# One change to a four-layer attention kernel: its hand-made order is laid out with other costs and constraints, and the rows of maxima travel in two transfers instead of four

## The chip, the cores and the metric

The kernel runs on one core of one Trainium2 chip. The time is the device time of one execution in microseconds, and the number to predict is the median over several executions of the changed kernel. The engines are TensorE (PE in the profile, its weight loads PEld), VectorE (DVE), ScalarE (ACT), GpSimd (POOL) and SyncE (SP), which here only issues transfers.

## The reference

The input x is [4, 2048, 256] in fp32. Four layers follow, each with a residual and a layer norm without parameters:

```
x = x + attn0(norm(x))      # one head, key and value width 64, causal, T = 2048, biases
x = x + ffn0(norm(x))       # fp8-quantised input and weight, 256 -> 256, plus bias
x = x + attn1(norm(x))      # 16 heads of width 16, rotary embedding, causal
x = x + ffn1(norm(x))       # sigmoid(xr Wr) * (relu(xk Wk)^2 Wv), xr and xk mix x with the row before
```

Causal softmax takes scores minus the row's maximum. The 16-head attention over 4 x 2048 positions is most of the work.

## The kernel before, in words

The sequence is cut into 16 chunks of 512 positions (4 batches x 4). Each chunk has a first stage (layer norms 0, 1 and 2, the single-head attention, the fp8 layer, the projections Q, K and V of the 16-head attention, rotary embedding, and the writing of Q, K and V to DRAM), and a last stage (output projection, layer norm 3, the last layer). Between them lie 64 blocks (batch, group of 4 heads, chunk of queries) of the 16-head attention. A block first makes the scores with queries on the partitions, only to find each row's maximum: TensorE writes them into PSUM (job `max`, L1905 and L1912) and VectorE reduces them (`max d`, L1639 and L1643). The maxima are joined and split in two fp16 parts (`nmax`, L1652, L1655, L1656), turned by TensorE (`turnmax`, L1922), copied to SBUF (`turnmax d`, L1668) and sent by SyncE into two extra contraction rows of the query tile `qst` (`rows`, L1096). Then TensorE makes the scores with keys on the partitions, the maximum already subtracted by those extra rows (`scores`, L1937 and L1944), ScalarE takes the exponential (`exp`, L1402), and TensorE multiplies by the values (`values`, L1959).

A layer norm is three jobs: `stats` on VectorE (L1501, L1504), `root` on GpSimd (L1186, L1188), `norm` on VectorE: four tensor_scalar instructions of 128x256 from SBUF to SBUF (L1523). `mix` (L1694) is two instructions with two SBUF operands. GpSimd adds biases (L1200 `bias0`, L1230 `bias`), sums probabilities (`sum0`, L1216 to L1224), finishes the rotary embedding (`roped`, L1242), squares (L1270) and adds residuals (L1237, L1275). After four of the first `root` jobs GpSimd also fills the key tiles (`pool.memset(kst...)`, L1193, eight instructions); these belong to no job.

Order. When the program is built, `schedule()` lays out some 10,000 jobs by a greedy simulation: `Order.run` calls `go` for each stretch of 3 us, with a random set of weights on the kinds of job drawn from the next number of the list `SEEDS`. In `go` each engine takes, of the jobs that are possible now, the one of lowest key plus weight. A job has an engine, a key, a time for which it holds its engine, a latency `lat` until its successors see it, the jobs it comes after, and what PSUM banks it takes or frees. The result is one fixed list of jobs for each engine, and the program emits instructions in exactly that order, with semaphore waits only for data and buffers. So an engine never passes over a job that isn't ready. The planned times themselves appear nowhere in the program, save in `repeats()`, which puts filler matmuls (L1727) where TensorE is planned to be idle for long.

SyncE issues all transfers of the main part from one queue in its own planned order. `put` (L1054, three transfers) and `put v` (L1060, four) write Q, K and V to DRAM, `load k`, `load q` (L1080, two each) and `load v` (L1088, one) read them back, `load x` (L1003) brings the next chunk.

Of the kernel before, what the change touches and what calls it, by code (L numbers as in the profile page):

```python
# [241 lines left out]
def max_pieces(i, c, g):  # L242
# [3 lines left out]
    if c == i // TPC and i % TPC == 1:  # L246
# [25 lines left out]
SEEDS = (405, 334, 333, 23, 291, 224, 511, 412, 119, 511, 511, 412, 255, 426, 355, 304, 119, 477, 180, 347, 49,  # L272
# [40 lines left out]
FAR_M, FAR_S = 2, 2  # L313
scored, paired = [], []


class State:


    def __init__(self, left, listed, jobs):  # L320
        self.left = left
        self.ready = {e: [] for e in ("PE", "DVE", "ACT", "POOL", "SP")}
        for name in listed:
            if not left[name]:
                self.ready[jobs[name][0]].append(name)
        self.ready_at = dict.fromkeys(listed, 0.0)
        self.free_at = dict.fromkeys(self.ready, 0.0)
        self.order = {e: [] for e in self.ready}
        self.vacant = [0.0] * 8
        self.home, self.tenants, self.start = {}, {}, {}  # L330
        self.now, self.mode, self.todo = 0.0, None, len(listed)


class Order:
# [47 lines left out]
    def go(self, state, then, number, until, weights, stick, patience):  # L382
# [4 lines left out]
        now, mode, todo = state.now, state.mode, state.todo  # L387

        def possible(name):

            at, claim = ready_at[name], jobs[name][5]
            if claim == "D":
                return max(at, min(max(vacant[n], vacant[n + 1]) for n in HOMES[claim]))
            return max(at, sorted(vacant[n] for n in HOMES[claim])[claim == "E"]) if claim else at

        while todo and now < until:
            nxt = 1e18
            moved = False
            for e in ready:
# [45 lines left out]
                free_at[e] = end  # L445
                if free:
# [14 lines left out]
        state.now, state.mode, state.todo = now, mode, todo  # L461


def chunk_jobs(o, b, q):
# [25 lines left out]
    add("SP", "load x", c, key() - (60.0 if b else 1e4), 0.1, ("store x2", p2), ("norm", p2 and (2, *p2)), lat=9.0 if c == (0, 1) else 4.0)  # L490
# [28 lines left out]
    add("SP", "rows0", c, key(), 0.2, ("turnmax0 d", c), ("rows0", p), last, lat=2.9)  # L519
# [34 lines left out]
    add("SP", "store x2", c, key(), 0.1, ("addf", (*c, 0)), ("addf", (*c, 1)), lat=3.0)  # L554
# [8 lines left out]
    for bl in range(4):  # L563
# [5 lines left out]
        add("SP", "put", (*c, bl), key(0.9), 0.5, ("res", (*c, bl)), lat=4.0)  # L569
# [3 lines left out]
    add("SP", "put v", c, key(), 0.4, ("v1", (*c, 0)), ("v1", (*c, 1)), lat=4.0)  # L573
# [8 lines left out]
def head_jobs(o, b, hg, q):  # L582
# [4 lines left out]
    for load in KEYS.loads(*me):  # L587
        old = KEYS.old[load]
        add("SP", "load k", load, pos - LEAD - 25, 0.15, ("put", (b, load[3], 2 * (hg // 2) + 1)),
            *[job for reader in (KEYS.readers(old) if old else []) for job in scored_with(*reader)], lat=4.5)  # L590
    slot = block_before(b, hg, q, QRING)
    add("SP", "load q", me, pos - LEAD - 25, 0.15, ("put", (b, q, 2 * (hg // 2))),
        *(scored_for(*slot) if slot else []), lat=4.5)
    for load in VALUES.loads(*me):
        old = VALUES.old[load]
        add("SP", "load v", load, pos - 25, 0.1, ("put v", (b, load[3])),
# [21 lines left out]
    add("SP", "rows", me, end - 20, 0.3, ("turnmax d", me), lat=2.6)  # L618
# [27 lines left out]
    add("SP", "put att", me, end + 2, 0.1, ("out", me), lat=3.0)  # L646


def tail_jobs(o, b, q):
# [12 lines left out]
    add("SP", "load x2", c, key(), 0.1, ("store x2", c), ("store y", p2),  # L662
        *[("put", (0, NQ - 1, bl)) for bl in (2, 3) if c in ((0, 0), (0, 1))], lat=4.0)
    add("SP", "load att", c, key(), 0.1, *[("put att", (b, hg, q)) for hg in range(NHG)],
# [38 lines left out]
    add("SP", "store y", c, key(), 0.1, ("addv", (*c, 0)), ("addv", (*c, 1)), lat=3.0)  # L703
# [107 lines left out]
def build(nc, x_in, y_out, w):  # L811
    ctx = ExitStack()
    with ctx:
# [81 lines left out]
        nmaxb = sb("nmaxb", [P, MAXROWS, 2, HG // 2, TPC], F16)  # L895
# [72 lines left out]
        def rows_written(wt, b, hg, q):  # L968
            n = block_no(b, hg, q)
            wt.wait_ge(f"rows {n % QRING}", 64 * (n // QRING + 1))  # L970
# [23 lines left out]
        def _(sp):  # L994
# [24 lines left out]
            for kind, item in ORDER["SP"]:  # L1019
# [70 lines left out]
                elif kind == "rows":  # L1090
                    n = block_no(*item)
                    wt.job("turnmax d", item)
                    for odd in range(2):
                        for row in range(MAXROWS):
                            at = 8 * (2 * row + odd)
                            sp.dma_start(qst[HALF * odd + PROWS + row:HALF * odd + PROWS + row + 1, n % QRING, :, :],  # L1096
                                         nmaxT1[at:at + 8, n % 2, :]).then_inc(S[f"rows {n % QRING}"], 16)
# [347 lines left out]
        def _(dve):  # L1445
# [36 lines left out]
            for kind, item in ORDER["DVE"]:  # L1482
# [163 lines left out]
                elif kind == "nmax":  # L1646
# [4 lines left out]
                    for odd in range(2):  # L1651
# [3 lines left out]
                    link(dve.tensor_scalar(nmaxb[:, 0, :, :, :], nmax1[:, :, :, :], 1.0 / UNIT1, None, ALU.mult))  # L1655
                    ins = dve.scalar_tensor_tensor(out=nmaxb[:, 1, :, :, :].rearrange("p o g t -> p (o g t)"),  # L1656
                                                   in0=nmax1[:, :, :, :].rearrange("p o g t -> p (o g t)"), scalar=1.0 / UNIT1,
# [396 lines left out]
```

## Time and profile before

| | |
|---|---|
| median of 3 runs | 2310.23 us (2308.37 to 2310.39) |
| the profiled execution's own time | 2312.3 us |
| its span, first to last instruction | 2310.4 us |
| granted TensorE clock, mean | 0.993 |
| SyncE transfers of the rows of maxima (L1096) | 256, of 2 KB each |

The span is 1.9 us less than the profiled execution's own time, and that time is 2.1 us over the median. Engine busy shares are averages over the whole span. A matmul's end is modelled by the profiler, so a busy TensorE isn't TensorE at its peak. In the rows below an instruction group of the timeline is merged: "1.38 ... x4" is 1.38 us from the first start to the last end of four instructions. A bracket at the end is the idle time of that engine before the group and what ended it.

### The profile page before, as it was taken

The page shows a single profiled execution, that of the slowest core. Times are in us where ns is not written, and L with a number is a line of the kernel's source. Part 1 is how long each engine was busy: PE and PEld are TensorE (multiplying, and loading weights), DVE is VectorE, ACT ScalarE, POOL GpSimd, SP SyncE. Part 2 cuts the span into 40 slices and gives each one's busy share as a digit, 9 for nine tenths or more (in the row PEclk, how much of TensorE's full clock was granted, in tenths as well). Part 3 has the DMA queues.
Part 4 walks back from the last instruction along what each step waited for, and adds up shares of the span by engine and source line. Part 5 has one row for each costly group of instructions (what it writes and reads, how often), then busy time and mean ns, then how long its engine had stood idle before and what let it go on. Part 6 is the DMA issues. An engine that isn't in the chain of part 4 may idle for free. (4 is left out here: it accounts for less than half of the span.)

```text
span 2310.4 us, 50495 instructions
## 1 busy us (share of the span) xinstructions
PE 2207.4 (96%) x19196; PEld 1022.9 (44%) x19196; DVE 2005.4 (87%) x4326; ACT 1506.5 (65%) x2753; POOL 529.9 (23%) x528
## 2 busy tenths in 40 slices
PE   7799999999999999999999999999999999999998
PEld 4455543343444444443354545444354444342444
DVE  6678999998988998898998989899988899999942
ACT  2234567767756777766846677667675677778764
POOL 6454220212223020312124112230222300000012
PEclk9999999999999999999999999999999999999999
DMA  2412312120211221120121212122021131010110
GB/s 52 120 59 72 109 37 77 34 65 15 60 45 47 75 73 50 54 71 15 51 68 47 76 50 80 33 59 58 20 68 55 32 90 53 21 43 25 30 49 30
DMA packets 185883, 125.29 MB, mean 54 GB/s; under 512 B 84912, under 2 KB 185392, under 8 KB 185648
## 3 DMA queue, kind: packets, MB, share of 16 engines
q1 hardware_dynamic: 184880, 121.16, 18.9%
q8 instruction: 157, 2.57, 0.5%
q10 hardware_dynamic: 768, 0.92, 0.1%
q14 instruction: 78, 0.64, 0.1%
HBM read 62.20 MB, written 59.24 MB: 53 GB/s over the span
## 5 line engine op out<-in xcount | busy, mean ns | idle before, releaser
L1639 DVE TENSOR_REDUCE mx<-psum 128x1 f32<-128x512 f32 (+2 forms) x2304 | 1291.3, 621 | 87.0 <-PE psum L1905 55.2
L1402 ACT ACTIVATE probs<-psum 128x512 f32<-128x512 f32 x2176 | 1136.1, 609 | 316.2 <-PE psum L1937 185.4
L1959 PE MATMUL psum<-probs,vs 128*17 128x512 f32 (+3 forms) x5120 | 573.7, 535 | 1.2 <-ACT probs L1402 1.0
L1905 PE MATMUL psum<-kst,qst 48*128 48x512 f16 (+3 forms) x2560 | 428.1, 350 | 26.8 <-DVE mx L1639 12.8
L1937 PE MATMUL psum<-qst,kst 50*128 50x512 f16 (+3 forms) x2560 | 419.7, 350 | 27.9 <-DVE mx L1639 7.7
L1905 PEld LDWEIGHTS psum<-kst,qst 48*128 48x128 f16 x2560 | 127.3, 93 | 346.8 <-ACT probs L1402 131.3
L1937 PEld LDWEIGHTS psum<-qst,kst 50*128 50x128 f16 x2560 | 125.0, 93 | 306.2 <-ACT probs L1402 115.4
L1959 PEld LDWEIGHTS psum<-probs,vs 128*17 128x17 f32 x5120 | 96.6, 96 | 165.9 <-issue 139.7
L1912 PE MATMUL psum<-maskq,identh 64*128 64x128 bf16 (+1 forms) x2048 | 125.2, 202 | 0.0
L1186 POOL TENSOR_SCALAR vare<-mv 128x4 f32<-128x4 f32 x64 | 14.6, 229 | 471.7 <-DVE mv L1504 471.7
L1944 PE MATMUL psum<-maskk,identh 64*128 64x64 bf16 (+1 forms) x2048 | 113.0, 202 | 0.0
L1944 PEld LDWEIGHTS psum<-maskk,identh 64*128 64x128 bf16 x2048 | 95.3, 95 | 33.3 <-issue 0.7
L1912 PEld LDWEIGHTS psum<-maskq,identh 64*128 64x128 bf16 x2048 | 95.6, 95 | 31.4 <-issue 0.6
L1872 PE MATMUL psum<-wqk,xnT 128*128 128x512 f32 x224 | 104.5, 604 | 1.3 <-DVE roped L1622 0.9
L1275 POOL TENSOR_TENSOR xp<-xp,gate 128x512 f32<-128x512 f32 x32 | 40.7, 1275 | 228.9 <-DVE gate L1702 228.9
L1242 POOL TENSOR_TENSOR roped<-rcos,roped 128x512 f32<-128x512 f32 x56 | 72.8, 1307 | 87.9 <-DVE roped L1622 87.9
L1356 ACT ACTIVATE probs<-psum 128x1024 f32<-128x1024 f32 x48 | 49.1, 1023 | 66.8 <-PE psum L1813 66.4
L1523 DVE TENSOR_SCALAR xn<-xs,mv,rstd 128x256 f32<-128x256 f32 x192 | 85.4, 506 | 6.4 <-POOL rstd L1188 6.0
L1643 DVE TENSOR_REDUCE mx<-psum 128x2 f32<-128x512 f32 x128 | 82.7, 681 | 8.3 <-PE psum L1912 8.1
L1501 DVE BATCH_NORM_STATS2 stats<-xs 128x6 f32<-128x256 f32 x192 | 67.0, 410 | 24.1 <-DMA xs<-x_in 13.6
L1222 POOL TENSOR_TENSOR sums<-sums,probs 128x512 f32<-128x512 f32 (+1 forms) x64 | 72.4, 1131 | 64.8 <-ACT probs L1356 42.9
L1745 PE MATMUL psum<-ident,xn 128*128 128x128 f32 x512 | 69.1, 281 | 14.3 <-DVE xn L1523 13.9
(173 smaller groups left out, 2757.4 us busy)
## 6 DMA issues: line engine op xcount, KB each, us to landing
qk_dram<-parts SPq DMA_DIRECT2D x168, 128.0 KB
qst<-qk_dram SPq DMA_DIRECT2D x128, 96.0 KB, 2.3
kst<-qk_dram SPq DMA_DIRECT2D x128, 96.0 KB, 2.3
v_dram<-vst SPq DMA_DIRECT2D x64, 136.0 KB, 4.0
vs<-v_dram SPq DMA_DIRECT2D x64, 136.0 KB, 2.1
xs<-x_in SPq DMA_DIRECT2D x16, 512.0 KB, 3.9
x_dram<-xs SPq DMA_DIRECT2D x16, 512.0 KB, 3.2
att_dram<-ast SPq DMA_DIRECT2D x64, 128.0 KB, 2.0
```

The source lines that it names most:

```text
L1222: pool.tensor_tensor(sums0[:, off:CH], sums0[:, off:CH], even, ALU.add).then_inc(S["chain s"], 1)
L1242: pool.tensor_tensor(into[:, t, :], rcos[:, t % 2, :], into[:, t, :], ALU.add).then_inc(S["roped"], 1)
L1402: act.activation(dst, src, ACT.Exp, scale=DK1 ** -0.5 / LIFT ** 2).then_inc(S["exp"], 1)
L1523: ins = dve.tensor_scalar(dst[:, t, :], src[:, t, :], mv[:, at, t, 0:1], rstd[:, at, t:t + 1], ALU.subtract, ALU.mult)
L1639: ins = dve.tensor_reduce(mx1[:, n % 2, 2 * g + odd, tile % TPC, c:c + 1], bank(src, at, at + cols), AX.X, ALU.max)
L1643: ins = dve.tensor_reduce(mx1[:, n % 2, odd:HG:2, i % TPC, c], tiles(bank(src, 0, cols * len(pieces)), cols), AX.X, ALU.max)
L1872: ins = pe.matmul(home(kind, item), xnTs[lane(b, q)][:, c, P * t:P * (t + 1)], wqk1[:, c, :], start=(c == 0), stop=(c == DC - 1))
L1905: ins = pe.matmul(two[odd][:, at:at + cols], qst[rows, qslot, pair, P * (tile % TPC):P * (tile % TPC + 1)], kst[rows, kslot, pair, 0:cols] ...
L1912: ins = pe.matmul(two[odd][:, at + cols - P + HALF * part:at + cols], identh[rows, part, :], maskq[rows, part, HALF * part:P], start=False ...
L1937: ins = pe.matmul(two[odd][:, at:at + cols], kst[rows, kslot, pair, keys], qst[rows, qslot, pair, CH - cols:CH], start=True, stop=not diag ...
L1944: ins = pe.matmul(two[odd][:, at:at + upto], identh[rows, part, :], maskk[rows, part, 0:upto], start=False, stop=(part == 1))
L1959: ins = pe.matmul(bank(7, off, CH, rows=VW, row=32 * h), vtile[:, h, :], probs[:, HG * (step_no(b, hg, k) % PSTEPS) + h, at:at + CH - off] ...
```

## The change

Three things are changed. First, the order's constraints: VectorE jobs of the kinds in `SHARED` (`norm`, `mix`, `nmax`) are possible only when GpSimd is free in the plan, and GpSimd jobs are possible only after the last of those has ended (`port`). Nothing of this is a wait in the program; it only moves jobs in the lists. Second, the time for which a transfer job holds SyncE in the plan. Third, the rows of maxima: the fp16 parts are laid out as (odd, part, head pair x tile), so that one transfer of 16 source rows writes both extra rows of a half of `qst`. `SEEDS` is another list (753 numbers for 752), so the order of all jobs on all engines is another one.

```diff
+SHARED = ("norm", "mix", "nmax")
...
         def possible(name):
 
             at, claim = ready_at[name], jobs[name][5]
+            if name[0] in SHARED and jobs[name][0] == "DVE":
+                at = max(at, free_at["POOL"])
+            if jobs[name][0] == "POOL":
+                at = max(at, port)
...
                 end = start + time
                 free_at[e] = end
+                if e == "DVE" and name[0] in SHARED:
+                    port = end
...
-    add("SP", "load x", c, key() - (60.0 if b else 1e4), 0.1, ...
+    add("SP", "load x", c, key() - (60.0 if b else 1e4), 0.45, ...
-    add("SP", "rows0", c, key(), 0.2, ..., lat=2.9)
+    add("SP", "rows0", c, key(), 1.35, ..., lat=2.9)
-        add("SP", "put", (*c, bl), key(0.9), 0.5, ("res", (*c, bl)), lat=4.0)
+        add("SP", "put", (*c, bl), key(0.9), 1.87, ("res", (*c, bl)), lat=3.0)
-    add("SP", "put v", c, key(), 0.4, ..., lat=4.0)
+    add("SP", "put v", c, key(), 2.1, ..., lat=4.0)
-        add("SP", "load k", load, pos - LEAD - 25, 0.15, ...   # load q alike
+        add("SP", "load k", load, pos - LEAD - 25, 0.85, ...
-        add("SP", "load v", load, pos - 25, 0.1, ...           # store x2, put att, load x2, load att, store y alike
+        add("SP", "load v", load, pos - 25, 0.45, ...
-    add("SP", "rows", me, end - 20, 0.3, ("turnmax d", me), lat=2.6)
+    add("SP", "rows", me, end - 20, 1.35, ("turnmax d", me), lat=2.1)
...
-        nmaxb = sb("nmaxb", [P, MAXROWS, 2, HG // 2, TPC], F16)
+        nmaxb = sb("nmaxb", [P, 2, MAXROWS, HG // 2 * TPC], F16)
...
                     for odd in range(2):
-                        for row in range(MAXROWS):
-                            at = 8 * (2 * row + odd)
-                            sp.dma_start(qst[HALF * odd + PROWS + row:HALF * odd + PROWS + row + 1, n % QRING, :, :],
-                                         nmaxT1[at:at + 8, n % 2, :]).then_inc(S[f"rows {n % QRING}"], 16)
+                        first = HALF * odd + PROWS
+                        sp.dma_start(qst[first:first + MAXROWS, n % QRING, :, :],
+                                     nmaxT1[16 * odd:16 * (odd + 1), n % 2, :]).then_inc(S[f"rows {n % QRING}"], 16)
...
-                    link(dve.tensor_scalar(nmaxb[:, 0, :, :, :], nmax1[:, :, :, :], 1.0 / UNIT1, None, ALU.mult))
-                    ins = dve.scalar_tensor_tensor(out=nmaxb[:, 1, :, :, :]..., in0=nmax1..., in1=nmaxb[:, 0, :, :, :]...,
+                    of = nmax1[:, :, :, :].rearrange("p o g t -> p o (g t)")
+                    link(dve.tensor_scalar(nmaxb[:, :, 0, :], of, 1.0 / UNIT1, None, ALU.mult))
+                    ins = dve.scalar_tensor_tensor(out=nmaxb[:, :, 1, :], in0=of, scalar=1.0 / UNIT1, in1=nmaxb[:, :, 0, :],
                                                    op0=ALU.mult, op1=ALU.subtract)
```

The semaphore of a block's rows now counts to 32 instead of 64, and the transpose of `nmaxb` reads the new layout.

## Rows read from the trace of the kernel before

**Rows 1.** The page, part 1: busy us, share of the span, instructions.
```profile
PE 2207.4 (96%) x19196; PEld 1022.9 (44%) x19196; DVE 2005.4 (87%) x4326; ACT 1506.5 (65%) x2753; POOL 529.9 (23%) x528
```
**Rows 2.** Stretches: us, busy PE, PEld, DVE, ACT, POOL, PEclk, DMA share, GB/s.
```profile
0.00:200.00 200.00, 166.74 (x1043) 93.96 (x1043) 138.77 (x327) 59.51 (x86) 105.65 (x124) 0.94 0.28 75
200.00:2200.00 2000.00, 1942.33 (x17515) 877.08 (x17515) 1829.52 (x3916) 1386.87 (x2559) 403.74 (x384) 1.00 0.19 53
```
**Rows 3.** Stretches, line L1523 (norm) alone: us, busy DVE, PEclk, DMA share, GB/s.
```profile
0.00:200.00 200.00, 32.87 (x44) 0.94 0.28 75
200.00:2310.00 2110.00, 84.76 (x212) 1.00 0.19 52
```
**Rows 4.** Timeline, VectorE: a norm with nothing beside it, one with company.
```profile
95.82 1.38 DVE L1523 TENSOR_SCALAR xn<-xs,mv,rstd 128x256 f32<-128x256 f32 x4
46.79 5.91 DVE L1523 TENSOR_SCALAR xn<-xs,mv,rstd 128x256 f32<-128x256 f32 x4 [1.48 <-POOL rstd L1188]
```
**Rows 5.** Timeline, GpSimd, beside that second norm.
```profile
46.71 1.84 POOL L1193 MEMSET kst<- 128x1024 f16 x2
48.51 1.30 POOL L1216 TENSOR_TENSOR sums<-probs 128x512 f32<-128x512 f32 x1
...
51.30 1.26 POOL L1224 TENSOR_TENSOR sums<-sums,probs 128x512 f32<-128x512 f32 x1
```
**Rows 6.** Groups by line: mix and the fp16 part of the maxima.
```profile
L1694 DVE SCALAR_TENSOR_TENSOR xrk<-x3T,mu,xrk 128x512 f32<-128x512 f32 x64 | 47.8, 790 | 13.2 <-ACT xrk L1423 13.2
L1655 DVE TENSOR_SCALAR nmaxb<-nmax 128x16 f16<-128x16 f32 x64 | 17.6, 275 | 2.2
```
**Rows 7.** The same lines: ns minimum/median/maximum of one instruction.
```profile
L1694 DVE SCALAR_TENSOR_TENSOR xrk<-x3T,mu,xrk x64: 729/742/1749, 327.2 to 2294.2; 128x512 f32<-128x512 f32 x64
L1655 DVE TENSOR_SCALAR nmaxb<-nmax x64: 174/175/2257, 134.3 to 2215.7; 128x16 f16<-128x16 f32 x64
```
**Rows 8.** Line L1193, the key tiles' filling.
```profile
L1193 POOL MEMSET kst<- x8: 951/951/952, 22.4 to 74.2; 128x1024 f16 x8
```
**Rows 9.** Timeline, VectorE and GpSimd: GpSimd starts inside VectorE's job.
```profile
977.09 3.43 DVE L1523 TENSOR_SCALAR xn<-xp,mv,rstd 128x256 f32<-128x256 f32 x4
977.25 2.46 POOL L1200 TENSOR_TENSOR xs<-xs,boc 128x1024 f32<-128x1024 f32 x1 [1.01 <-DVE xn L1523]
```
**Rows 10.** Timeline, SyncE, 92 to 112 us.
```profile
95.57 3.97 SPq L1054 DMA_DIRECT2D qk_dram<-xp  x6
99.64 2.09 SPq L1080 DMA_DIRECT2D qst<-qk_dram  x4
...
105.57 1.85 SPq L1080 DMA_DIRECT2D kst<-qk_dram  x4
107.51 0.40 SPq L1003 DMA_DIRECT2D xs<-x_in  x1
```
**Rows 11.** Timeline, VectorE and TensorE, what waits for that load.
```profile
101.73 1.15 DVE L1561 TENSOR_REDUCE mx<-psum 128x1 f32<-128x384 f32 x2
112.75 1.40 DVE L1501 BATCH_NORM_STATS2 stats<-xs 128x6 f32<-128x256 f32 x4 [9.88 <-DMA xs<-x_in]
115.86 1.22 PE L1872 MATMUL psum<-wqk,attT 128*128 128x512 f32 x1 [9.01 <-DVE xrk L1622]
```
**Rows 12.** Timeline, SyncE: one block's rows (L1096), one chunk's (L1039).
```profile
1032.93 2.72 SPq L1096 DMA_DIRECT2D qst<-nmaxT  x4
249.50 1.35 SPq L1039 DMA_DIRECT2D nm<-nmaxT  x2
```
**Rows 13.** Waits of TensorE: total us, times, longest.
```profile
PE psum L1745 <- DVE xn L1523: 13.9, 6, 4.0
PE psum L1905 <- DVE mx L1639: 12.8, 37, 2.0
PE psum L1937 <- DMA qst<-nmaxT: 4.5, 6, 1.2
```

More of the change, by code:

```diff
@@ L269 @@
 STRETCH, AMPLITUDE = 3.0, 60.0
-SEEDS = (405, 334, 333, 23, 291, 224, 511, 412, 119, 511, 511, 412, 255, 426, 355, 304, 119, 477, 180, 347, 49,
[35 rows of a table removed]
+SEEDS = (158, 23, 200, 40, 361, 477, 216, 312, 314, 23, 426, 121, 412, 283, 327, 412, 412, 427, 157, 41, 180,
[35 rows of a table added]
 HOMES = {"D": (0, 2, 4), "E": (0, 1, 2, 3, 4, 5, 6), "P": (6, 5, 4, 3, 2, 1, 0), "O": (6,), "V": (7,)}
 FAR_M, FAR_S = 2, 2
+SHARED = ("norm", "mix", "nmax")
 scored, paired = [], []
@@ L330, in __init__ @@
         self.home, self.tenants, self.start = {}, {}, {}
-        self.now, self.mode, self.todo = 0.0, None, len(listed)
+        self.now, self.mode, self.todo, self.port = 0.0, None, len(listed), 0.0
 class Order:
@@ L386, in go @@
         vacant, home, tenants, order = state.vacant, state.home, state.tenants, state.order
-        now, mode, todo = state.now, state.mode, state.todo
+        now, mode, todo, port = state.now, state.mode, state.todo, state.port
         def possible(name):
             at, claim = ready_at[name], jobs[name][5]
+            if name[0] in SHARED and jobs[name][0] == "DVE":
+                at = max(at, free_at["POOL"])
+            if jobs[name][0] == "POOL":
+                at = max(at, port)
             if claim == "D":
@@ L460, in go @@
                 now = max(now, nxt)
-        state.now, state.mode, state.todo = now, mode, todo
+        state.now, state.mode, state.todo, state.port = now, mode, todo, port
 def chunk_jobs(o, b, q):
@@ L488, in both @@
         return (("turned", (ln, *c)),)
-    add("SP", "load x", c, key() - (60.0 if b else 1e4), 0.1, ("store x2", p2), ("norm", p2 and (2, *p2)), lat=9.0 if c == (0, 1) else 4.0)
+    add("SP", "load x", c, key() - (60.0 if b else 1e4), 0.45, ("store x2", p2), ("norm", p2 and (2, *p2)), lat=9.0 if c == (0, 1) else 4.0)
     norm(0, ("load x", c))
@@ L518, in chunk_jobs @@
     add("DVE", "turnmax0 d", c, key(), 0.13, ("turnmax0", c), ("rows0", same), free=("turnmax0", c))
-    add("SP", "rows0", c, key(), 0.2, ("turnmax0 d", c), ("rows0", p), last, lat=2.9)
+    add("SP", "rows0", c, key(), 1.35, ("turnmax0 d", c), ("rows0", p), last, lat=2.9)
     pairs = TPC * (q + 1) // 2
@@ L553, in chunk_jobs @@
     norm(2, ("addf", (*c, 0)), ("addf", (*c, 1)))
-    add("SP", "store x2", c, key(), 0.1, ("addf", (*c, 0)), ("addf", (*c, 1)), lat=3.0)
+    add("SP", "store x2", c, key(), 0.45, ("addf", (*c, 0)), ("addf", (*c, 1)), lat=3.0)
     turn(2, ("QK0", c), ("V0", c))
@@ L572, in chunk_jobs @@
         add("ACT", "v1", (*c, n), key(), 0.5, ("V1", (*c, n)), ("put v", p), free=("V1", (*c, n)))
-    add("SP", "put v", c, key(), 0.4, ("v1", (*c, 0)), ("v1", (*c, 1)), lat=4.0)
+    add("SP", "put v", c, key(), 2.1, ("v1", (*c, 0)), ("v1", (*c, 1)), lat=4.0)
 POS, _at = {}, 0
@@ L588, in head_jobs @@
         old = KEYS.old[load]
-        add("SP", "load k", load, pos - LEAD - 25, 0.15, ("put", (b, load[3], 2 * (hg // 2) + 1)),
+        add("SP", "load k", load, pos - LEAD - 25, 0.85, ("put", (b, load[3], 2 * (hg // 2) + 1)),
             *[job for reader in (KEYS.readers(old) if old else []) for job in scored_with(*reader)], lat=4.5)
     slot = block_before(b, hg, q, QRING)
-    add("SP", "load q", me, pos - LEAD - 25, 0.15, ("put", (b, q, 2 * (hg // 2))),
+    add("SP", "load q", me, pos - LEAD - 25, 0.85, ("put", (b, q, 2 * (hg // 2))),
         *(scored_for(*slot) if slot else []), lat=4.5)
@@ L595, in head_jobs @@
         old = VALUES.old[load]
-        add("SP", "load v", load, pos - 25, 0.1, ("put v", (b, load[3])),
+        add("SP", "load v", load, pos - 25, 0.45, ("put v", (b, load[3])),
             *[job for reader in (VALUES.readers(old) if old else []) for job in summed_with(*reader)], lat=4.0)
@@ L645, in head_jobs @@
         free=("turnout", me))
-    add("SP", "put att", me, end + 2, 0.1, ("out", me), lat=3.0)
+    add("SP", "put att", me, end + 2, 0.45, ("out", me), lat=3.0)
 def tail_jobs(o, b, q):
@@ L661, in tail_jobs @@
     lent = (0, NQ - 1) if c == (0, 0) else None
-    add("SP", "load x2", c, key(), 0.1, ("store x2", c), ("store y", p2),
+    add("SP", "load x2", c, key(), 0.45, ("store x2", c), ("store y", p2),
         *[("put", (0, NQ - 1, bl)) for bl in (2, 3) if c in ((0, 0), (0, 1))], lat=4.0)
-    add("SP", "load att", c, key(), 0.1, *[("put att", (b, hg, q)) for hg in range(NHG)],
+    add("SP", "load att", c, key(), 0.45, *[("put att", (b, hg, q)) for hg in range(NHG)],
         ("turn", p and ("A", *p)), lat=4.0)
@@ L702, in tail_jobs @@
         add("POOL", "addv", (*c, n), key(), 1.24, ("gated", (*c, n)))
-    add("SP", "store y", c, key(), 0.1, ("addv", (*c, 0)), ("addv", (*c, 1)), lat=3.0)
+    add("SP", "store y", c, key(), 0.45, ("addv", (*c, 0)), ("addv", (*c, 1)), lat=3.0)
 def schedule():
@@ L969, in rows_written @@
             n = block_no(b, hg, q)
-            wt.wait_ge(f"rows {n % QRING}", 64 * (n // QRING + 1))
+            wt.wait_ge(f"rows {n % QRING}", 32 * (n // QRING + 1))
         def v_loaded(wt, b, hg, q, c):
@@ L1654, in _ @@
                     link(ins)
-                    link(dve.tensor_scalar(nmaxb[:, 0, :, :, :], nmax1[:, :, :, :], 1.0 / UNIT1, None, ALU.mult))
-                    ins = dve.scalar_tensor_tensor(out=nmaxb[:, 1, :, :, :].rearrange("p o g t -> p (o g t)"),
-                                                   in0=nmax1[:, :, :, :].rearrange("p o g t -> p (o g t)"), scalar=1.0 / UNIT1,
-                                                   in1=nmaxb[:, 0, :, :, :].rearrange("p o g t -> p (o g t)"),
+                    of = nmax1[:, :, :, :].rearrange("p o g t -> p o (g t)")
+                    link(dve.tensor_scalar(nmaxb[:, :, 0, :], of, 1.0 / UNIT1, None, ALU.mult))
+                    ins = dve.scalar_tensor_tensor(out=nmaxb[:, :, 1, :], in0=of, scalar=1.0 / UNIT1, in1=nmaxb[:, :, 0, :],
                                                    op0=ALU.mult, op1=ALU.subtract)
@@ L1922, in _ @@
                     pe.transpose(home(kind, item).bitcast(BF16)[0:32, 0:P],
-                                 nmaxb[:, :, :, :, :].rearrange("p r o g t -> p (r o g t)").bitcast(BF16), identb[:, :]
+                                 nmaxb[:, :, :, :].rearrange("p o r n -> p (o r n)").bitcast(BF16), identb[:, :]
                                  ).then_inc(S["turnmax"], 1)
```

70 rows, old and new, of the table SEEDS are left out of this document.

## The prediction

> **What bounds the kernel now.** I read the page's busy shares first: TensorE 96%, VectorE 87%, GpSimd 23% [rows 1]. By stretch they differ. In the first 200 us VectorE is busy 138.8 us (69%) and TensorE 166.7, with GpSimd at 105.7, more than half; from 200 to 2200 us VectorE is at 1829.5 of 2000 (91%) and TensorE at 1942 [rows 2]. So the start is a stretch of serial chains (load, stats, root, norm, turn, projections) in which nobody is full, and the middle is a stretch in which VectorE and TensorE feed each other through PSUM and a microsecond that VectorE loses is mostly lost. The waits of TensorE say the same: its longest waits are for `norm` (13.9 us in 6 waits) and for the reductions of maxima (12.8 in 37) [rows 13]. Since the order is a fixed list, a late job also holds all that is listed behind it.
>
> **Part 1, norm, mix and nmax apart from GpSimd.** Four instructions of a norm take 1.38 us undisturbed; the norm at 46.79 takes 5.91 [rows 4], and beside it GpSimd works without a pause [rows 5]: each VectorE instruction waits for a GpSimd one to end. The loss over the program: in the first 200 us 44 instructions, 11 norms, are 32.87 us against 11 x 1.38 = 15.2, a loss of 17.7; later 53 norms are 84.76 against 73.1, a loss of 11.6 [rows 3]. For mix the mean is 790 ns against a median of 742, 64 times: 3.1 us; for the fp16 part 275 against 175, 64 times: 6.4 us [rows 6, 7]. Sum: 38.8 us of VectorE, 17.7 of it at the start and 21.1 later.
>
> Not all of it goes. (a) The key tiles' filling belongs to no job, so the plan doesn't know of it. Eight fills of 951 ns, two behind each of four roots [rows 8], each time as a norm starts: the undisturbed loss of such a norm is some 1.5 us (1.84 for the two fills, as in rows 5, less the first norm instruction). 4 x 1.5 = 6.0 us stays. (b) The plan holds GpSimd back while VectorE is in such a job, but no wait in the program does. Where GpSimd's job becomes ready by itself during it, the program starts it at once. The norm at 977.09 shows this: GpSimd starts 0.16 us into it, and it takes 3.43 instead of 1.38 [rows 9]. Going through the timeline I find seven disturbed jobs out of 32 of which that is true, with 10.7 us (3.1 at the start, 7.6 later), and one more, like that at 977, where a norm directly follows a norm, 2.0 us. What is left that the new order can avoid is 38.8 - 6.0 - 10.7 - 2.0 = 20.1 us: 8.6 at the start, 11.5 later.
>
> What it is worth: at the start a held norm is still in a serial chain and VectorE has 31% idle time [rows 2], so part of the loss becomes a planned delay; I take 0.7, 6 us. In the middle VectorE is the fuller engine and does reductions meanwhile; I take 0.95, 11 us. Bounds: nothing, if the holds cost what they save, and 38.8 us if even (a) and (b) vanish. Cost of the holding itself: 64 norms, 32 mixes and 64 nmax are 160 jobs; at a GpSimd share of 0.23 [rows 1] and half of a 1.3 us instruction [rows 5] left each time, 160 x 0.23 x 0.65 = 24 us if nothing covered it. The reductions of maxima in the list do cover it in the middle. I take 3 us, with 0 and 24 as ends.
>
> The Trainium skill has a rule that bears on (b): in "SBUF — State Buffer", section "Who interferes with whom", the shared port pair is an exclusive lock and "issue order, not op shape, decides who blocks". By that rule a plan without a wait separates nothing by itself; the trace agrees in the norm at 977 (3.43 us) [rows 9]. Taken strictly, it is the second rival below.
>
> **Part 2, the real hold of transfers.** In the old plan a `put` holds SyncE 0.5 us and a `load k` 0.15. The trace: six transfers of L1054 take 3.97 us, so 0.66 each and 2.0 for a put; a load's two take 0.9 to 1.05 [rows 10]. So SyncE's list is made for a queue that is never behind, and in the trace it is behind. The case that costs is `load x` of chunk 3, issued at 107.51, directly behind sixteen issues for q and k, four groups of four [rows 10]. VectorE is done at 102.88 and waits 9.88 us for it, and TensorE 9.01 [rows 11]; the device stands still. That transfer waits for the third norm of chunk 1, which ends at 97.20 (95.82 + 1.38) [rows 4], and in the plan it has by far the lowest key of SyncE's jobs. With real holds the queue is behind at 97.2 in the plan too, so `load x` goes ahead of the loads of k and q, behind one put at most (2.0 us): issue by 99.2, landing some 5 us after (112.75 - 107.51 = 5.2), at 104.4. The wait falls from 9.9 to 1.5. TensorE's 9.0 is what sets the end: 7.5 to 8.5 gained, I take 8. Bounds: 0, if another order of the start leaves it behind, and 9.9. The sixteen loads come 0.4 us later each; they feed head blocks that start dozens of us after. Elsewhere no wait of this size for a transfer stands in the trace, so I cost the other holds at nothing; the ends are a gain of 4.5 us, all that TensorE waits for rows [rows 13], and a loss of 9.9, one more stall like this one.
>
> **Part 3, rows in two transfers.** Four issues hold SyncE 2.72 us; two issues of the sister transfer of layer 0, which also go from several source rows to two target rows, hold it 1.35 [rows 12]. The last row starts 1.37 us earlier. TensorE waits for these rows six times, 4.5 us in all, at most 1.2 [rows 13], so each wait is shorter than what goes: 4 us gained, with 0 (if the new order uses up the slack) and 4.5 as ends. 64 x 1.37 = 88 us of SyncE's queue are freed, and whatever stands behind rows in its list is issued 1.4 us earlier; nothing waits for most of it. The two VectorE instructions keep size and count; their target now has two pieces of 8 instead of 16 in a row, at 175 ns an instruction hardly above its fixed part. I take 0 (ends: none, and 64 x 0.1 us).
>
> The Trainium skill, "DMA: Bandwidth & Descriptors", section "Why a DMA increments its semaphore by 16 and not by 1", says that a transfer runs on the largest number of engines up to 16 that divides both sides' slowest dimension. By it the old transfer of 8 source rows could use 8 and the new one, with 2 target rows, only 2, which speaks against the merging. The row of the sister transfer shows only the issue (1.35 us). An estimate from the trace of the price, 16 pieces instead of 8 in one transfer at the old 0.68 us issue: below 0.7 us a block, still less than the 1.37 gained, so the sum stays.
>
> **Sum.** 6 + 11 - 3 + 8 + 4 = 26 us. The whole order being another one adds a scatter that I can't sign; single accidents of the present order cost 9 and 4 us [rows 11, 13], so I allow 8 each way. Jobs, their number and their durations are otherwise the same. The profiled execution goes from 2312.3 to 2286.3 (its span from 2310.4 to 2284.4); it lies 2.1 above the median, which gives 2310.2 - 26 = 2284 for the median.
>
> **Rivals.**
> 1. *More goes than I think.* The list being right, jobs behind a delayed one are no longer late, and the clashes of kind (b) occur more seldom since all jobs near a norm have moved: 20.1 + 10.7 at nearly full price, plus 8 and 4: 2310 - 43 = 2267. For it: the largest gaps of TensorE at the start lie directly behind disturbed norms, 4.0 us the longest of them [rows 13]. Against: kind (b) needs a wait to go.
> 2. *The separation doesn't hold in the run* (the change doesn't do what it says). GpSimd starts when its data are there, new clashes come for old. Part 1 gives 0 and costs 3, the transfers give 12: 2301. For it: rows 9. Against: in 24 of 32 cases GpSimd was already at work as VectorE came, and that the list can avoid.
> 3. *The load of chunk 3 stays behind*, for instance since its norm comes later in the new list: 2284 + 8 = 2292.
> 4. *Slower: the holds move the norms.* A norm held until GpSimd is idle opens the chain norm, turn, ScalarE's copy, projection; at the start GpSimd is busy 53% of the time [rows 2] and VectorE has nothing to fill in. If the holds are not covered (24 us) and the reductions ahead of norms make TensorE wait for them (its 12.8 us [rows 13] doubled), against 12 from transfers and nothing from part 1: 2310 + 24 + 13 - 12 = 2335 at worst, 2320 half-way. It decides from where uncovered holds exceed 27 us, the sum of the gains, which is above the 24 of its upper end; so it needs both.
>
> **How the numbers follow.** My forecast 0.52; rival 1 0.15; rival 2 0.15; rival 3 0.10; rival 4 0.08. The range 2266 to 2303 takes in rivals 1 to 3 and leaves out rival 4 and tails. The forecast's own range is 2276 to 2292. This kernel's runs lie 0.1% apart, so a difference under 0.2%, 4.6 us, can't be told from none. Faster by more: all of the forecast, rivals 1 and 3 and most of 2, 0.88; same 0.05 (the tail of 2 and of 4); slower 0.07.
>
> **What would show it.** Line L1523: mean of the xs group down from 506 ns to about 440, its start stretch from 32.9 us to about 24; L1655 down to about 215 ns. The wait of `stats` for `xs<-x_in` below 4 us in total. TensorE's wait for `qst<-nmaxT` near 0 and two issues in about 1.35 us a block. Busy time of TensorE in matmuls unchanged, its idle time and VectorE's down. Wrong would be: VectorE's L1523 as slow as before (then rival 2), the stall of 9 us near 100 us still there (rival 3), or more waits of TensorE for `xn` and `mx` than 27 us together (rival 4).

## The result, and the profile after

| | before | after |
|---|---|---|
| median of four runs | 2310.1 us | 2294.5 us |
| profiled execution's span | 2310.4 us | 2290.7 us |
| forecast | | 2284 (2266 to 2303) |

The ratio after to before is 0.9936, 95% interval 0.9918 to 0.9953: 15.6 us or 0.64% faster, clear of no change. The jobs stand in another order, but the work is the same: the page's first row, as [rows 1], shows the engines' busy times within 2.2 us of before (the weight loads 3.3 us less), so the difference is idle time. One run of e4_apart (6313.8 us), one of e12_rows_loadx (3029.8 us) and one of the kernel before beside e9_all_old (11690.6 us) were slow ones and stand in no median or ratio below.

The page after, part 1:
```profile
PE 2205.2 (96%) x19207; PEld 1019.6 (45%) x19207; DVE 2004.0 (87%) x4326; ACT 1506.6 (66%) x2753; POOL 530.1 (23%) x528
```
By stretch, as [rows 2] and then, for the norm's line alone (now L1531), as [rows 3]:
```profile
0.00:200.00 200.00, 173.62 (x1104) 95.95 (x1105) 153.72 (x348) 60.65 (x88) 111.06 (x128) 0.97 0.30 77
200.00:2200.00 2000.00, 1951.12 (x17642) 881.05 (x17641) 1827.47 (x3930) 1397.58 (x2580) 402.31 (x383) 1.00 0.19 53
```
```profile
0.00:200.00 200.00, 31.14 (x44) 0.97 0.30 77
```
By VectorE the gain is made at the start: it is busy 15 us more in the first 200 us and 2 us less in the 2000 us after them. TensorE is busy 7 us more at the start and 9 us more in the middle [rows 2], so a part is made there too. The norms at the start are hardly faster, 31.1 us for 32.9 [rows 3].

The load of chunk 3, the timeline of SyncE and then of VectorE, as [rows 10, 11]:
```profile
98.00 2.86 SPq L1063 DMA_DIRECT2D qk_dram<-xp  x4
100.96 0.41 SPq L1012 DMA_DIRECT2D xs<-x_in  x1
101.47 0.92 SPq L1089 DMA_DIRECT2D kst<-qk_dram  x2
```
```profile
99.27 1.38 DVE L1531 TENSOR_SCALAR xn<-xs,mv,rstd 128x256 f32<-128x256 f32 x4
...
107.38 1.41 DVE L1509 BATCH_NORM_STATS2 stats<-xs 128x6 f32<-128x256 f32 x4 [1.05 <-DMA xs<-x_in]
```
It is issued 0.3 us after the norm it waits for has ended (99.27 + 1.38 = 100.65), ahead of the loads of k and q, and VectorE waits 1.05 us instead of 9.88. The use comes 6.4 us after the issue, later than the 5.2 us of before; the wait is short also because this list has more work ahead of the `stats`.

The rows of maxima, SyncE's timeline, as [rows 12]:
```profile
1012.57 1.35 SPq L1104 DMA_DIRECT2D qst<-nmaxT  x2
```
TensorE's waits (total us, times, longest), as [rows 13]:
```profile
PE psum L1752 <- DVE xn L1531: 15.0, 8, 3.2
PE psum L1912 <- DVE mx L1647: 11.0, 28, 2.7
...
PE psum L1929 <- DVE nmaxb L1665: 2.7, 3, 2.1
```
The wait for `qst<-nmaxT` is gone from the list. The wait for norms is not smaller, and a new one stands there, of the transpose of the maxima for their fp16 parts. The groups that GpSimd disturbs, as [rows 6] with the two norm groups:
```profile
L1531 DVE TENSOR_SCALAR xn<-xs,mv,rstd 128x256 f32<-128x256 f32 x192 | 81.9, 487 | 5.4 <-POOL rstd L1196 5.4
L1701 DVE SCALAR_TENSOR_TENSOR xrk<-x3T,mu,xrk 128x512 f32<-128x512 f32 x64 | 48.8, 806 | 14.5 <-ACT xrk L1431 14.5
L1531 DVE TENSOR_SCALAR xn<-xp,mv,rstd 128x256 f32<-128x256 f32 x64 | 22.9, 420 | 5.3 <-POOL rstd L1196 5.3
L1664 DVE TENSOR_SCALAR nmaxb<-nmax 128x16 f16<-128x16 f32 x64 | 19.2, 301 | 2.2
```
From here on *the loss* of a kernel is what VectorE loses beside GpSimd, by such rows: the two norm groups' busy time less 64 x 1.38 us, plus 64 times what the mean of mix is over 742 ns and that of the fp16 part over 175 ns. After: 16.5 + 4.1 + 8.1 = 28.7 us. Before, by the same count, 39.0 (its two norm groups are 85.4 and 32.4 us): by this count 10.3 us went, not the 20.1 that I had forecast. The last stage's norms (xp) lose almost nothing now, the first stage's nearly as much as ever, and mix and the fp16 part lose more than before.

The count leaves out two groups that lose time in the new order and lost none before. First those of before, then those of after:
```profile
L1543 DVE TENSOR_SCALAR wqk<-wqk,wnorm 128x512 f32<-128x512 f32 x2 | 0.9, 484 | 0.0
L1656 DVE SCALAR_TENSOR_TENSOR nmaxb<-nmax,nmaxb 128x16 f16<-128x16 f32 x64 | 11.2, 175 | 2.2
```
```profile
L1551 DVE TENSOR_SCALAR wqk<-wqk,wnorm 128x512 f32<-128x512 f32 x2 | 4.9, 2493 | 0.0
L1665 DVE SCALAR_TENSOR_TENSOR nmaxb<-nmax,nmaxb 128x16 f16<-128x16 f32 x64 | 13.2, 207 | 2.2
```
The first is the scaling of the weights, whose kind isn't in `SHARED`. It starts at 29.36 us, and two biases of GpSimd (L1208) run from 29.14 to 33.98 beside it. The second is the other instruction of the fp16 parts. Together they take back 6.0 of the 10.3 us, and VectorE's busy time as a whole is only 1.4 us less than before (2004.0 for 2005.4). What VectorE lost beside GpSimd was moved more than it was removed.

One of the jobs that lose more, the timeline of VectorE, of GpSimd and of TensorE:
```profile
800.68 0.27 DVE L1660 TENSOR_REDUCE nmax<-mx 128x8 f32<-128x32 f32 x2
800.98 2.23 DVE L1664 TENSOR_SCALAR nmaxb<-nmax 128x16 f16<-128x16 f32 x1
```
```profile
800.84 2.35 POOL L1238 TENSOR_TENSOR xs<-xs,bf 128x1024 f32<-128x1024 f32 x1 [2.90 <-DVE xn L1531]
```
```profile
803.57 0.22 PE L1929 MATMUL psum<-identb,nmaxb 128*32 128x128 bf16 x1 [2.13 <-DVE nmaxb L1665]
```
A norm ends, GpSimd's bias waits for just that norm and starts 0.16 us into `nmax`; the 175 ns instruction takes 2.23 us and TensorE stands for 2.13. The plan has the bias behind `nmax`; the program has nothing that makes it wait.

### The profile page after: what moved, and what is told of

Its sections match the earlier page's. It is cut to its first block, busy times and chain, and to the rows that moved or that the text cites. A ratio compares the mean times of both kernels' runs of the same rounds, so it can differ in the third digit from the quotient of the medians.

```text
span 2290.7 us, 50374 instructions
## 1 busy us (share of the span) xinstructions
PE 2205.2 (96%) x19207; PEld 1019.6 (45%) x19207; DVE 2004.0 (87%) x4326; ACT 1506.6 (66%) x2753; POOL 530.1 (23%) x528
## 4 chain that ended last, share of the span: by engine, by line
PE 73%; DVE 19%; ACT 4%; issue 2%; DMA 1%; POOL 1%; SPq 1%; POOLq 0%; DVEq 0%; ACTq 0%
PE psum L1966 18%; DVE mx L1647 11%; PE psum L1912 10%; PE psum L1944 9%; PE psum L1879 5%; PE psum L1752 3%; PE psum L1843 3%; ACT probs L1410 3%; PE psum L2017 3%; PE psum L2005 2%; PE psum L1814 2%; PE psum L1986 2%; PE psum L1997 2%; PE psum L1783 2%; PE psum L1900 2%
## 5 line engine op out<-in xcount | busy, mean ns | idle before, releaser
L1944 PE MATMUL psum<-qst,kst 50*128 50x512 f16 (+3 forms) x2560 | 421.6, 349 | 21.3 <-ACT probs L1410 7.1
L1919 PE MATMUL psum<-maskq,identh 64*128 64x64 bf16 (+1 forms) x2048 | 125.4, 202 | 0.0
L1951 PEld LDWEIGHTS psum<-maskk,identh 64*128 64x128 bf16 x2048 | 94.5, 95 | 32.4 <-issue 0.6
L1278 POOL TENSOR_TENSOR attT<-attT 128x512 f32<-128x512 f32 x32 | 33.3, 1041 | 285.5 <-ACT attT L1447 285.5
L1531 DVE TENSOR_SCALAR xn<-xs,mv,rstd 128x256 f32<-128x256 f32 x192 | 81.9, 487 | 5.4 <-POOL rstd L1196 5.4
```

What stands on the lines that cost most here:

```text
L1531: ins = dve.tensor_scalar(dst[:, t, :], src[:, t, :], mv[:, at, t, 0:1], rstd[:, at, t:t + 1], ALU.subtract, ALU.mult)
L1919: ins = pe.matmul(two[odd][:, at + cols - P + HALF * part:at + cols], identh[rows, part, :], maskq[rows, part, HALF * part:P], start=False ...
L1944: ins = pe.matmul(two[odd][:, at:at + cols], kst[rows, kslot, pair, keys], qst[rows, qslot, pair, CH - cols:CH], start=True, stop=not diag ...
L1951: ins = pe.matmul(two[odd][:, at:at + upto], identh[rows, part, :], maskk[rows, part, 0:upto], start=False, stop=(part == 1))
```

## The experiments

Each ran beside the kernel before on one chip (e9_all_old on another chip than the others), where that kernel had medians of 2310.3 to 2311.9 us; ratios are to that kernel, with their 95% intervals. The changed kernel has only its four runs of the result, 2292.5 to 2297.9 us.

**Two transfers alone** (e1_rows). The kernel before with the third part of the diff, and no other.

> The kernel before with one part of the change alone: the rows of maxima in two transfers; the order of all jobs is that of before. My theory: TensorE's waits for these rows (4.5 us in the trace of before) nearly vanish, since the last row is issued 1.37 us earlier; time 2310.1 - 3.5 = 2306.6. Rival (hidden anyway: the order gives the slack back at the next wait): 2310 +- 1, though the waits are gone from the trace. The other side (two target rows land later than before): the waits grow, 2312 or more.

Measured: 2307.3 us, ratio 0.9985 (0.9976 to 0.9993), 3 to 3.5 us. The rows take 1.36 us and TensorE's wait for them is gone from its list of waits:
```profile
1030.50 1.36 SPq L1095 DMA_DIRECT2D qst<-nmaxT  x2
```
My theory holds; the gain isn't given back. The rows land earlier too, by the whole of the 1.3 us: from the start of a block's first issue to the last write of its semaphore the traces have 3.73 us before and 2.40 here (medians of 64 blocks), and from the start of the last issue 1.68 and 1.74 us.

**The load alone** (e2_loadx).
```diff
 PLAN, ORDER = schedule()
+_sp = ORDER["SP"]
+_at = _sp.index(("load x", (0, 3)))
+_sp.insert(_at - 8, _sp.pop(_at))
```


> The kernel before with one transfer moved in SyncE's list: the load of x for chunk 3 stands ahead of the eight jobs that load q and k (sixteen issues) instead of behind them; all other lists are untouched. My theory: VectorE's wait of 9.9 us near 103 us falls to about 1.5, TensorE's 9.0 to below 1, and since nothing later waits on that side the whole is kept: 2310.1 - 8 = 2302. Rival (the stall is given back, because the loads of q and k or the clashes behind it decide): 2306 to 2310.

Measured: 2303.4 us, ratio 0.9972 (0.9962 to 0.9983), 6.5 to 7 us of the 8. The timeline of SyncE and VectorE shows the missing part:
```profile
98.92 0.96 SPq L1006 DMA_DIRECT2D xs<-x_in  x1
```
```profile
105.91 1.41 DVE L1504 BATCH_NORM_STATS2 stats<-xs 128x6 f32<-128x256 f32 x4 [3.50 <-DMA xs<-x_in]
```
The issue was within 0.3 us of what I had worked out, but from its start to the use are 7.0 us, not 5.2, and the wait is 3.5 instead of 1.5; TensorE's wait falls from 9.0 to 2.6 us, not below 1. Why that landing took longer isn't tested; the sixteen loads for q and k, which went ahead of it before, are now issued behind it and share the DMA engines with it (busy to 86% over those 7.0 us).

**Both** (e12_rows_loadx).

> The kernel before with both transfer parts and nothing else: rows of maxima in two transfers, and the load of x for chunk 3 ahead of the loads of q and k. All other lists are those of before. My theory: the two gains add, since they lie in different places (3.0 us by the first alone, 6.9 by the second): 2310.3 - 10 = 2300.4. Then the new list of jobs is worth the rest of the change, 2300.4 - 2294.5 = 6 us. Rival (they share a wait): 2303.

Measured: 2301.5 us, ratio 0.9959 (0.9943 to 0.9974), 9.5 to 9.6 us. The two ratios multiplied are 0.9957: they add, as far as three runs show; the interval takes in the rival's 2303 too. The loss is 39.0 us as before. The rest of the change, from 0.9959 to 0.9936, is 5 us by the ratios and 7 by the medians.

**The load put back in the changed kernel** (e5_back; the same edit with `_at + 8`).

> The changed kernel with that one load put back behind the eight jobs that load q and k; the part undone in the other order. My theory: the wait of some 9 us near 105 us is back: 2294.5 + 7 to 9 = 2302. Rival (the new list has slack for it): 2295 to 2297.

Measured: 2300.8 us, ratio 0.9951 (0.9937 to 0.9964), slower than the changed kernel by 6.3 us of median and by 3.5 us of ratio; the intervals of the two ratios overlap. Between runs with the same mean granted TensorE clock, 0.996, it is 3.7 us (2296.3 against 2292.5 and 2292.6), so I take some 4 us, under the 7 to 9 expected. VectorE's wait is back, but smaller, since this list has its stats later:
```profile
112.20 1.41 DVE L1512 BATCH_NORM_STATS2 stats<-xs 128x6 f32<-128x256 f32 x4 [5.99 <-DMA xs<-x_in]
```

**The fills moved** (e3_fills). On the changed kernel:
```diff
-                    elif pieces < KRING:
-                        for _ in range(2):
-                            pool.memset(kst[:, pieces, :, :], UNIT1).then_inc(done, 1)
...
                 elif kind == "wsquare":       # at its end; the other four at the end of "wroot"
+                    for piece in range(KRING // 2):
+                        pool.memset(kst[:, piece, :, :], UNIT1).then_inc(done, 1)
```


> The changed kernel with the eight fills of the key tiles taken from behind four roots, where a norm starts, and put where GpSimd is idle: four behind the squares of the weights, four behind the root of the weights. My theory: these four norms lose 1.4 to 1.7 us less each, 6 us of VectorE in serial chains; 2294.5 - 5 = 2289.5. Rival (VectorE has idle time at the start, so the loss is covered, or the sums that follow the fills clash earlier instead): 2293 to 2295.

Measured: 2288.7 us, ratio 0.9906 (0.9894 to 0.9919), 5.8 us under the changed kernel; the loss falls from 28.7 to 23.9. All four runs lie under the changed kernel's four, so the rival falls: even at the start, where VectorE has idle time, this loss is paid. The 5.8 us for 4.8 of loss look like a microsecond for each, but with the scatter of the runs the price is known only roughly.

**A real wait** (e4_apart). On the changed kernel, `BEHIND` gives each GpSimd job the last VectorE job of `SHARED` that the plan starts before it:
```diff
+BEHIND, _port = {}, None
+for _name in sorted(ORDER["POOL"] + [n for n in ORDER["DVE"] if n[0] in SHARED],
+                    key=lambda n: (PLAN.start[n], PLAN.jobs[n][0] == "POOL")):
+    if PLAN.jobs[_name][0] == "POOL":
+        BEHIND[_name] = _port
+    else:
+        _port = _name
...
             for kind, item in ORDER["POOL"]:
+                if BEHIND[kind, item]:
+                    wt.job(*BEHIND[kind, item])
```


> The changed kernel in which the separation is made real: every GpSimd job first waits for the last norm, mix or nmax that the plan has before it. Lists are those of the changed kernel. My theory: in the changed kernel's trace ten disturbed jobs lose 13.2 us because GpSimd starts inside VectorE's job by itself; that goes, and GpSimd's jobs come 0.5 to 1.4 us later, most of them with slack; 2294.5 - 7 = 2287. Rival (the lock only moves the delay from VectorE to GpSimd's successors, or GpSimd waits for late norms): 2294 or more.

Measured: 2273.8 us, ratio 0.9844 (0.9832 to 0.9857), 21 us under the changed kernel where I expected 7. The norm groups, the place near 800 us again (VectorE, then GpSimd), and TensorE's wait for norms:
```profile
L1540 DVE TENSOR_SCALAR xn<-xs,mv,rstd 128x256 f32<-128x256 f32 x192 | 73.1, 443 | 5.4 <-POOL rstd L1205 5.4
L1540 DVE TENSOR_SCALAR xn<-xp,mv,rstd 128x256 f32<-128x256 f32 x64 | 22.0, 407 | 5.4 <-POOL rstd L1205 5.4
```
```profile
786.93 0.17 DVE L1673 TENSOR_SCALAR nmaxb<-nmax 128x16 f16<-128x16 f32 x1
787.14 0.18 DVE L1674 SCALAR_TENSOR_TENSOR nmaxb<-nmax,nmaxb 128x16 f16<-128x16 f32 x1
```
```profile
787.39 2.37 POOL L1247 TENSOR_TENSOR xs<-xs,bf 128x1024 f32<-128x1024 f32 x1 [3.52 <-DVE nmaxb L1674]
```
```profile
PE psum L1761 <- DVE xn L1540: 4.5, 5, 2.0
```
GpSimd's bias now waits for the fp16 parts and `nmaxb` takes its 0.17 us; the bias starts 0.78 us behind the start of `nmax` (786.61) instead of 0.16. TensorE's wait for norms falls from 15.0 to 4.5 us. The loss is 6.8 + 0.3 + 2.5 = 9.6, down by 19.1, and the second instruction of the fp16 parts is back at 11.2 us, 2.0 less: again about one for one, and the holding of GpSimd costs nothing that can be seen. A part of the 21 us comes with a higher granted clock (the last section). I had counted only jobs into which GpSimd starts (13.2 us). The first norm of chunk 0's second layer, [rows 4, 5] in the kernel before, shows what else goes: with the wait only one of the sums behind the fills gets in its way, the two others come after it, and it takes 3.83 us for 5.91.

**The wait on the lists of before** (e8_before_apart).

> The kernel before, all its lists untouched, with the wait alone: every GpSimd job waits for the last norm, mix or nmax that the plan of before puts ahead of it. That plan knows nothing of the port. My theory: the jobs in which GpSimd starts inside VectorE's job go (10.7 us of loss) and those in which GpSimd was at work already stay, so 2310.3 - 9 = 2301. Rival (the wait was worth 20 us in the changed kernel because of the lock in general, not because of the list): 2290. Rival (a wait on a list that isn't made for it holds GpSimd's successors): 2310 or more.

Measured: 2298.2 us, ratio 0.9942 (0.9929 to 0.9956), 13 us. It lies between my 2301 and the rival's 2290, nearer to mine. But the loss is 21.3, down by 17.7 where I had expected 10.7, so the time came out near for the wrong reason: more goes than the jobs into which GpSimd starts, and here the price is 0.75 of it. The wait reaches the later GpSimd jobs beside a norm too, as in the example above; what stays (its norms are 76.6 and 26.8 us) is mostly jobs that find GpSimd at work.

**Wait and fills** (e6_both), on the changed kernel.

> The changed kernel with the wait and with the fills moved to where GpSimd is idle. My theory: the gains add, 20 us for the wait and 5.8 for the fills, since what is left of loss with the wait alone is 10.7 us, of which 6.1 stand beside the fills: 2274.5 - 6 = 2268.5. Rival (the start is then bound by something else): 2272 to 2275.

Measured: 2269.3 us, ratio 0.9821 (0.9807 to 0.9834), the fastest of all, 25 us under the changed kernel and 41 under the one before. The two gains add within the scatter, as expected. The loss is 1.7 + 0.1 + 2.6 = 4.4 us:
```profile
L1540 DVE TENSOR_SCALAR xn<-xs,mv,rstd 128x256 f32<-128x256 f32 x192 | 68.0, 415 | 5.3 <-POOL rstd L1205 5.3
L1540 DVE TENSOR_SCALAR xn<-xp,mv,rstd 128x256 f32<-128x256 f32 x64 | 22.0, 404 | 5.4 <-POOL rstd L1205 5.4
```

**Everything on the lists of before** (e9_all_old).

> All hand-made parts on the lists of before: rows in two transfers, the load for chunk 3 moved ahead, the wait for separation, the fills moved. Against the changed kernel with the wait and the fills (2269.3 us) only the list of jobs differs. My theory: the list laid out with the constraint is worth most together with the wait, because it has moved VectorE's jobs out of GpSimd's way (loss found at work: 21 us of VectorE in the lists of before, 7 in the new ones). Sum by the single runs: 2310.5 - 3 (rows) - 6.5 (load) - 13 (wait) - 5 (fills) = 2283, so the list is worth 14 us. Rival (the wait is all that matters, the new list is no better): 2270 to 2273.

Measured: 2286.5 us, ratio 0.9897 (0.9879 to 0.9914). Against 0.9821 the new lists are worth 17 us once the wait is there; the rival, 2270 to 2273, falls. The loss (17.5 against 4.4) is 13 us of it by the count, but the new lists pay 4.2 us more in the scaling of the weights, and VectorE's busy time differs by only 7.9 us (1985.6 against 1977.7). What the rest is stays open.
```profile
L1535 DVE TENSOR_SCALAR xn<-xs,mv,rstd 128x256 f32<-128x256 f32 x192 | 73.0, 442 | 7.0 <-POOL rstd L1200 6.7
L1535 DVE TENSOR_SCALAR xn<-xp,mv,rstd 128x256 f32<-128x256 f32 x64 | 26.8, 479 | 5.9 <-POOL rstd L1200 5.9
```

**Unsearched lists.** Three kernels with one number for every stretch of `SEEDS`, to part the constraint from the search.

> The changed kernel with an unsearched list: one number, 236, for every stretch in SEEDS. The constraint of separation is on. To be compared with u2_free_236. It will be much slower than before, since the search of SEEDS is missing: 2450 to 2550. My theory: the loss of norm, mix and nmax beside GpSimd is clearly less than in u2, by a third to a half, because only jobs that find GpSimd at work are held, not those into which it starts.

> The same unsearched kernel without the constraint of separation in the list (both conditions taken out of possible()), real holds and two transfers kept. My theory: the loss beside GpSimd is 35 to 50 us, as before the change (some 20% of such jobs disturbed, about GpSimd's share of the span); time within 15 us of u1 either way, since the rest of the list is another one too. Rival (the search of SEEDS, not the constraint, is what lowered the loss from 40 to 30 us): the same loss in u1 and u2.

> u1's lists with the wait: every GpSimd job waits for the last norm, mix or nmax that the plan has before it. My theory: loss beside GpSimd down to about 10 us, and the time 15 us or so under u1, since the lists are the same. Rival (the one-for-one gain in the changed kernel came from its tightly searched list): less than 5 us under u1.

| | loss | time | ratio |
|---|---|---|---|
| u1, constraint in the list | 21.1 us | 2482.1 | 1.0737 (1.0701 to 1.0774) |
| u2, no constraint | 25.8 us | 2466.0 | 1.0667 (1.0627 to 1.0708) |
| u3, u1 with the wait | 7.2 us | 2474.2 | 1.0703 (1.0672 to 1.0734) |

The norm groups of u1 and u2:
```profile
L1496 DVE TENSOR_SCALAR xn<-xs,mv,rstd 128x256 f32<-128x256 f32 x192 | 76.6, 461 | 9.0 <-POOL rstd L1161 5.0 <-PE psum L1717 3.9
L1496 DVE TENSOR_SCALAR xn<-xp,mv,rstd 128x256 f32<-128x256 f32 x64 | 22.0, 405 | 4.4 <-POOL rstd L1161 4.4
```
```profile
L1492 DVE TENSOR_SCALAR xn<-xs,mv,rstd 128x256 f32<-128x256 f32 x192 | 79.4, 474 | 9.9 <-POOL rstd L1157 7.6 <-PE psum L1713 2.3
L1492 DVE TENSOR_SCALAR xn<-xp,mv,rstd 128x256 f32<-128x256 f32 x64 | 24.5, 444 | 4.4 <-POOL rstd L1157 4.4
```
With the constraint the loss is a fifth lower, less than I expected, and the list without it was 16 us faster all the same: one pair can't part that from the scatter between lists. I had expected 35 to 50 us of loss in u2; at 25.8 it has less than the changed kernel (28.7), without any constraint. So it isn't shown that the constraint is what brought the loss down from 39.0. The scaling of the weights is beside GpSimd in both (4.7 and 4.9 us). The wait is worth 8 us for 13.9 of loss, 0.6 for one, between my 15 and the rival's 5, with two runs of each and overlapping intervals. What these lists do show is that a searched `SEEDS` is worth 170 us or more against this one number (2466 and 2482 against 2294.5), ten times what this change brings. With so few pairs it stays open how much of the 5 to 7 us of the new list is the constraint and how much the luck of another search.

## Why the prediction was right, and where it was off

The forecast said faster, with the time in the range; the time itself is 10.5 us over the likeliest value and outside the forecast's own range of 2276 to 2292. The two transfer terms were right in place and nearly in size; the largest term, the separation, came out at less than half, and the wide range covered that. Point by point:

- *The load of chunk 3, 8 us.* Right in place and mechanism: 6.5 us alone, some 4 when undone in the new list. The issue came where I had put it; the use came later after the issue than 5.2 us. No run changes the holds alone, so that they put the load ahead isn't shown; u1 and u2, other lists with the same holds, have no such stall either (VectorE waits for `xs<-x_in` 3.3 and 3.7 us in all, against 13.6 before).
- *Rows in two transfers, 4 us.* 3 to 3.5 us. The rule of the Trainium skill on how many engines a transfer uses (page "DMA: Bandwidth & Descriptors", section "Why a DMA increments its semaphore by 16 and not by 1") had spoken against it. The traces agree with the rule as to the numbers: a block's semaphore is written 36 times before, four times 8 + 1, and 6 times in e1_rows, two times 2 + 1, in each of the 64 blocks, which fits 8 engines and 2, each with one write, and one further write for each transfer. But a transfer on two lands only 0.06 us later after its issue (1.74 for 1.68 us), so the number of engines doesn't decide here.
- *Separation, 6 + 11 - 3 = 14 us.* 5 to 7 us. The step that failed is "what is left that the new order can avoid is 20.1 us": it was 10.3, and 4.3 with the two groups outside the count, which the forecast had put at no change. I had counted the seven jobs of kind (b) as a fixed remainder and all others as avoided. In the timeline of the new list there are ten of kind (b), 13.2 us, three of them a mix into which the rotary sums start, as at 839.58. That a VectorE job placed where the plan has GpSimd idle stands where GpSimd is about to start is my reading of it, not shown. Some jobs that find GpSimd at work are still there too, 6.7 us. The fills stayed, as said, with 9.1 us including the sums behind the second.
- *The price of a microsecond of loss.* I took 0.7 at the start and 0.95 later, less 3 for holding. On this list it was about 1 (e4_apart: 21.1 us of VectorE for 21; e3_fills, all at the start: 4.8 for 5.8), on the two others 0.75 and 0.6, and holding cost nothing that can be seen. With 4.3 us and a price of 1 the sum is 4.3 + 6.5 + 3 = 14, against a measured 15.6; with 10.3 it would be 20. The two profiled executions differ by 19.7, but they ran at mean granted clocks of 0.993 and 0.996.
- *Second rival, the separation doesn't hold in the run.* Half right. The rule of the Trainium skill cited for it (page "SBUF — State Buffer", section "Who interferes with whom": issue order decides who blocks) agrees with the runs: at 800.84 us GpSimd issues first and the 175 ns instruction takes 2.23 us, and a real wait is worth more than the whole change (21 us against 15.6).
- *What would show it.* L1523's first-stage mean came to 487 ns instead of 440, and L1655's rose from 275 to 301 instead of falling to 215: these two told the miss at once. VectorE's waits for `xs<-x_in` are 4.6 us in total where I had said below 4: 1.05 at the stall and 3.5 at the first load of all, which this change doesn't touch.

## What to carry to other kernels

A separation of two engines that only the planner knows moved clashes here more than it removed them: where the plan relies on an engine holding back, try a semaphore wait, which brought 8 to 21 us in three lists and had no cost that could be seen. Count what the engine loses over all its lines and not only over those that the change is about. Before trusting a hand-laid order, compare the plan's holds with the durations in the trace (here 0.15 us planned, 0.9 us real for a load) and look for work that no job of the plan stands for, like the fills. And cost an avoided stall by the kind of its cause (who was there first), since an edit may reach only one kind.

## What was unexpected of the hardware

The granted TensorE clock of the first 200 us is not the same in these kernels: 0.94 before [rows 2], 0.97 with the load moved alone, 0.97 after, 0.98 with the wait, and 0.99 with wait and fills (e6_both):
```profile
0.00:200.00 200.00, 185.72 (x1275) 105.63 (x1276) 150.31 (x382) 72.55 (x110) 116.80 (x133) 0.99 0.33 87
```
TensorE is busy 185.7 us there against 166.7 before: with fewer gaps it is less often at the lower of its two levels (1.2 and 2.4 GHz). A gap at the start may so be paid for a second time. The order isn't strict: e3_fills, with less loss than the changed kernel, has 0.96.

The clock also differs between runs of one kernel, and the time goes with it. The changed kernel took 2292.5 and 2292.6 us at a mean granted clock of 0.996, 2296.5 and 2297.9 at 0.993; the kernel before had medians of 2307.8 (3 runs) and 2310.7 (16 runs) at the same two. Compared at 0.996, the change is worth 15 us, e3_fills 5.9 us more, and e4_apart 16 us more (2276.4, one run) where the medians say 21. So about 5 of those 21 us went with the higher clock of its other runs (0.997 and 0.998), while the 5.9 us of e3_fills, for 4.8 of loss, did not.
